# An attention and expert kernel: expert products ahead of the maxima, first-layer tiles in 50 pairs, the second tile table in two parts

## The reference

```python
x = L0_attn_x                                   # (8, 512, 256)
xn = _layernorm(x, axis=-1)
x = x + _L0_attn_ref(xn, ...) + _L0_ffn_ref(xn, ...)
xn = _layernorm(x, axis=-1)
x = x + _L1_attn_ref(xn, ...) + _L1_ffn_ref(xn, ...)
return x
```

## Time and profile before

| what | value |
|---|---|
| median of 3 runs | 3600.68 us (3591.55 to 3601.14) |
| the profiled execution | 3600.47 us, its span 3598.5 us |
| TensorE busy | 2938.4 us, 82% of the span |
| VectorE busy | 2166.3 us, 60% |
| ScalarE, GpSimd busy | 1650.5 us, 1419.2 us |
| 317 to 1560 us | pairs 0 to 51 with the first layer's tiles |
| 1560 to 1708 us | pairs 52 to 63, plain, with the gathers of sequences 0 and 1 |
| 1708 to 2511 us | gqa blocks and the routing of the second layer |
| 2558 to 3419 us | pairs 138 to 177 with the second layer's tiles |

### The profile page before, as it was taken

How to read it: one execution, slowest core, us unless ns; L and a number is a source line. 1 busy time by engine, 2 the same in 40 slices (tenths; PEclk the granted TensorE clock), 3 DMA queues, 4 the chain that set the end, 5 groups by cost and what they waited for, 6 DMA issues and landing times. The chain is left out here.

```text
span 3598.5 us, 61920 instructions
## 1 busy us (share of the span) xinstructions
PE 2938.4 (82%) x21678; PEld 2372.1 (66%) x21678; DVE 2166.3 (60%) x6233; ACT 1650.5 (46%) x3466; POOL 1419.2 (39%) x2037
## 2 busy tenths in 40 slices
PE   4415989898988899878888888987888888888885
PEld 3304778777777787755666666665677777777764
DVE  4534776767766767656777777666444444443465
ACT  1203445444444445445655566555444444444453
POOL 4744424333333424266656565223121212122267
PEclk9998999999999999989999999999999999999999
DMA  8853656555655655522433333211554544444345
GB/s 274 294 190 127 231 187 231 219 223 196 238 212 210 237 207 218 212 71 40 111 83 97 95 96 92 82 67 38 188 187 156 196 166 182 175 173 177 141 95 117
DMA packets 193735, 587.54 MB, mean 163 GB/s; under 512 B 22984, under 2 KB 145808, under 8 KB 158608
## 3 DMA queue, kind: packets, MB, share of 16 engines
q1 hardware_dynamic: 156560, 532.40, 40.1%
q0 software_dynamic: 36864, 51.14, 7.0%
HBM read 456.99 MB, written 126.48 MB: 162 GB/s over the span
## 5 line engine op out<-in xcount | busy, mean ns | idle before, releaser
L1231 POOL TENSOR_TENSOR al<-t,ah 128x512 fp32r<-128x512 f32 x224 | 289.8, 1294 | 1288.8 <-ACT ah L1408 1288.8
L762 PE MATMUL bank<-xh,gu 128*128 128x256 f32 x3584 | 668.8, 292 | 98.6 <-DVE t L1673 93.1
L808 PE MATMUL bank<-masks_bf,ident_bf 128*128 128x128 bf16 (+1 forms) x2304 | 578.6, 251 | 56.9 <-ACT ksT L1490 21.9
L762 PEld LDWEIGHTS bank<-xh,gu 128*128 128x128 f32 x3584 | 531.6, 196 | 118.9 <-DVE t L1673 104.3
L1822 DVE TENSOR_REDUCE st<-bank 128x1 f32<-128x512 f32 (+3 forms) x1024 | 424.4, 481 | 243.1 <-PE bank L815 242.8
L1503 ACT ACTIVATE pt<-bank 128x512 f32<-128x512 f32 (+1 forms) x1152 | 513.2, 540 | 74.3 <-PE bank L818 72.2
L1408 ACT ACTIVATE ah<-t 128x512 fp32r<-128x512 f32 x224 | 141.4, 631 | 714.6 <-DVE t L1666 383.7
L818 PE MATMUL bank<-qaT,ksT 128*128 128x512 f32 (+3 forms) x1536 | 433.3, 390 | 0.0
L1820 DVE MAX8 top<-bank 128x8 f32<-128x512 f32 (+3 forms) x512 | 214.1, 483 | 352.3 <-PE bank L815 352.2
L815 PE MATMUL bank<-ksT,qsT 128*128 128x512 f32 (+3 forms) x1536 | 420.7, 380 | 0.0
L808 PEld LDWEIGHTS bank<-masks_bf,ident_bf 128*128 128x128 bf16 x2304 | 225.4, 98 | 294.1 <-issue 105.7
(11 more groups left out here) (248 smaller groups left out, 5321.4 us busy)
## 6 DMA issues: line engine op xcount, KB each, us to landing
gu<-wu_scratch SPq DMA_DIRECT2D x112, 2056.0 KB, 7.7
dn<-wd_scratch SPq DMA_DIRECT2D x112, 1024.0 KB, 9.5
xs<-xs_scratch SPq DMA_DIRECT2D x112, 264.0 KB, 9.2
ys_scratch<-yb SPq DMA_DIRECT2D x112, 256.0 KB, 9.9
raw<-in_gu SPq DMA_DIRECT2D x16, 1024.0 KB, 10.4
wu_scratch<-hi SPq DMA_DIRECT2D x16, 1024.0 KB, 5.5
wu_scratch<-lo SPq DMA_DIRECT2D x16, 1024.0 KB, 4.0
xs_scratch<-empty SPq DMA_DIRECT2D x32, 264.0 KB, 2.8
```

Source lines behind the costliest of these rows:

```text
L762: mm = pe.matmul(bank[:, TS * h:TS * (h + 1)], gu[:, col:col + P], x[s % 2][:, TS * k:TS * (k + 1)], start=(n == 0), stop=(n == len(terms) ...
L808: pe.matmul(bank[:, diag:diag + P * len(unit)], ident_bf[:, :], masks_bf[:, 0 if which == "q" else 1, 0:len(unit), :].rearrange("p n k -> ...
L1231: pool.tensor_tensor(em["al"][s % 2][:, m, :], em["t"][g % 2][:, :], em["ah"][s % 2][:, m, :].bitcast(F32), ALU.subtract).then_inc(al_read ...
```

## The change

Four things. On VectorE, `finish` no longer stands at the start of a tiled pair but at its end, ahead of `normalize` and `norm_heads`, and once more between slot 2 and `maxima`. The first layer's tiles run in pairs 0 to 49; the gathers of sequence 0 stand in pairs 51 to 54, those of sequence 1 in 55 to 62. The second table's last part (L599 to L608, the slots' compaction) is a function of its own, run in pair 137, and SP waits for the first two of its four steps only. `place` copies its 64 columns of PSUM to SBUF first and works from there, so that the bank is released after the copy.

```diff
-SPANS = ((0, 52), (138, 178))
+SPANS = ((0, 50), (138, 178))
+FIRST_GATHERS = 55
...
     def place(dve, chain, bank, big, k, to, rank_used, slot_ready):
-        before = bank[:, 64:96].rearrange("p (t e) -> p t e", e=E)
-        total = bank[:, 96:128].rearrange("p (t e) -> p t e", e=E)
+        taken = big[:, 1, 128:192]
+        before = taken[:, 0:32].rearrange("p (t e) -> p t e", e=E)
+        total = taken[:, 32:64].rearrange("p (t e) -> p t e", e=E)
+        dve.tensor_copy(taken, bank[:, 64:128]).then_inc(rank_used[0], 1)
         chain(dve.tensor_copy(base[:, 0, :], running[:, :]))
+        dve.wait_ge(*rank_used)
         for t in range(1, NT):
             chain(dve.tensor_tensor(base[:, t, :], base[:, t - 1, :], total[:, t - 1, :], ALU.add))
         chain(dve.tensor_tensor(running[:, :], base[:, NT - 1, :], total[:, NT - 1, :], ALU.add))
-        dve.tensor_tensor(base[:, :, :], before, base[:, :, :], ALU.add).then_inc(rank_used[0], 1)
-        dve.wait_ge(*rank_used)
+        chain(dve.tensor_tensor(base[:, :, :], before, base[:, :, :], ALU.add))
...
         dve.tensor_copy(table[:, 1, :], which[:, 0, :]).then_inc(tabled, 1)
+
+    def compact_slots(dve, chain, layer, scratch, tabled):
...
         chain(dve.tensor_copy(at[:, 0, :], own))
...
-                    sp.wait_ge(tabled, 4)
+                    sp.wait_ge(tabled, 2)
...
-                    if is_at(n + 1, "gqa") and loc(n + 1) == 0:
-                        gather(1, p // 2, p % 2)
-                    if is_at(n + 2, "gqa") and loc(n + 2) == 0 and p >= NP // 2:
+                    if em and ends_at[0] < G <= ends_at[0] + CHOICES[0]:
                         for i in range(2):
-                            gather(0, p - NP // 2, i)
+                            gather(0, G - ends_at[0] - 1, i)
+                    if em and 0 <= G - FIRST_GATHERS < NP:
+                        gather(1, (G - FIRST_GATHERS) // 2, (G - FIRST_GATHERS) % 2)
...
                 def pair_with_experts(G):
                     n, p = divmod(G, NP)
-                    finish()
                     if G:
                         heads_out(G - 1)
...
                     experts(G, 2)
+                    finish()
                     maxima(G + 1, range(NU))
                     shift(G + 1)
                     for q in range(3, 6):
                         experts(G, q)
+                    finish()
                     if is_at(n - 1, "spm") and p == 1:
-                        finish()
                         residual(n - 1)
...
-                    if G + 1 in ends_at:
-                        finish()
...
                         tile_table()
+                    if em and is_at(n - 2, "gqa") and loc(n - 2) == B - 1 and p == 1:
+                        compact_slots(dve, chain, 1, em["scratch"], tabled)
```

More of the change, by code:

```diff
@@ L572, in table_scratch, with tabulate_on @@
         }
-    def tabulate_on(dve, chain, layer, scratch, empty, cleared, tabled):
-        k = CHOICES[layer]
-        own = slots[layer][:, 0:B * NT, :].rearrange("p n k -> p (n k)")
+    def tabulate_on(dve, chain, scratch, empty, cleared, tabled):
         n, over, below, past = (scratch[name] for name in ("n", "over", "below", "past"))
-        which, at, beyond, move = (scratch[name] for name in ("which", "at", "beyond", "move"))
+        which = scratch["which"]
         dve.memset(empty[:, :, :], 0.0).then_inc(cleared, 1)
@@ L598, in tabulate_on @@
         dve.tensor_copy(table[:, 1, :], which[:, 0, :]).then_inc(tabled, 1)
+    def compact_slots(dve, chain, layer, scratch, tabled):
+        k = CHOICES[layer]
+        own = slots[layer][:, 0:B * NT, :].rearrange("p n k -> p (n k)")
+        n, at, beyond, move = (scratch[name] for name in ("n", "at", "beyond", "move"))
         chain(dve.tensor_copy(at[:, 0, :], own))
@@ L620, in _ @@
                 def _(dve):
-                    tabulate_on(dve, Chain(dve, step), layer, scratch, empty, cleared, tabled)
+                    chain = Chain(dve, step)
+                    tabulate_on(dve, chain, scratch, empty, cleared, tabled)
+                    compact_slots(dve, chain, layer, scratch, tabled)
                 @block.sync
@@ L1994, in tile_table @@
                         dve.wait_ge(moved[i], 16 * NP * (B // 2))
-                    tabulate_on(dve, chain, 1, em["scratch"], em["empty"], cleared, tabled)
+                    tabulate_on(dve, chain, em["scratch"], em["empty"], cleared, tabled)
                 def finals(b):
```

## The result

The changed kernel takes 3412.5 us (median of 4 runs, 3407.5 to 3419.2), the kernel before 3600.0 (4 runs, 3591.6 to 3601.1): ratio 0.949, 95% interval 0.946 to 0.951. Forecast were 3431 and a range of 3380 to 3500. The profiled execution has a span of 3409.0 against 3598.5, and a mean granted clock of 0.969 against 0.955.

What follows compares the result with a forecast made beforehand. TensorE's queue was taken as the kernel's clock, with its idle time and lowered clock in the tiled pairs to be won. Terms summed to -169.5 us from 3600.5, giving 3431 us; range 3380 to 3500.

Steps and rivals of the forecast that it cites:

- Product ahead of the maxima, second stretch: Pairs 138 to 177: TensorE's 39 waits of 2.39 us for VectorE's product go, -93 us.
- rival C: Late maxima make shift the wait in the second stretch and 22 first-stretch pairs: +80 us, 3511; chance 0.08.
- Clock there: Second stretch: without the 2.39 us waits the granted clock rises from 0.95 to 0.985, -26 us, bounds 0 and -37.
- Rival A: Idle time goes but the clock stays: 3467 us, or 3490 with half of the first stretch's 47 us; chance 0.20.
- The stretch's last pair: Pair 177: its last product comes ahead of the maxima, so TensorE's wait of 7.06 us goes, -7 us.
- The finish's cost in the second stretch: Finish ahead of normalize delays the next rows' transposes at five block starts, +7 us, bounds 0 and +41.
- First stretch: Product ahead of maxima -31 us, finish ahead of norm_heads -16, clock -10, normalize later at four block starts +8.
- 50 pairs for 52: First-layer tiles in two pairs fewer, gathers a pair earlier: some slow stacks beside gathers, +2 us, bounds -5 and +14.
- Waits that I said would be below 5 us: Sign of being right: TensorE's first-stretch waits on `al` and `yb`, 17.6 and 17.0 us before, fall below 5 us.
- The table in two: Second table's L599 to L608 go behind pair 137's maxima; TensorE's 5.87 us wait ends 3.5 us earlier, -3.5 us.
- place: One more copy frees its bank about 1 us earlier, but the next bank comes 0.2 later: 0, bounds -8 and +2.

Runs made afterwards that it cites:

- finish-only kernel: The kernel before with only the finish moves, ahead of the maxima and at the pair's end; 52 pairs, old gathers, table and place: 3431.0 us, ratio 0.954.

## Why the prediction came out as it did

*Product ahead of the maxima, second stretch (-93): right.* The waits went from 93.1 to 2.4 us. Nothing took their place, since the maxima had their slack and the shift its own. But that slack was read from a pair that doesn't set it: pair 154, at place 2, has a projection ahead of the turn of the shifted queries, which the 0.3 us (0.2 in rival C) leaves out. In the changed kernel there are 2.9 us in such pairs and 0.12 to 0.21 in the 20 pairs without a projection. That the shift was in time there is partly luck. The kernel with the product between maxima and shift and a short `al` shows the other side: rival C was a matter of some 0.6 us, and waits of 0.53 came of it.

*Clock there (-26): right in kind, and 10 us too small.* From shift 138 to 184 the time fell by 134.5 us and TensorE's idle time by 96.2 (foretold: 93); of the other 38.3 about 2.5 are the 15 matmuls that the cut at shift 138 puts on its other side, and the rest, 36, is the clock, near the bound of 37. I had taken it that waits of 1 us would hold it at 0.985. They do not: half clock fell from 88.9 to 10.2 us, and the finish-only kernel has none at all between 139 and 177. Rival A, by which the clock would stay, is refuted: twice over by the line taken out and put in, and by the shorter waits without any fall. With it falls, for this kernel, the rule of the Trainium skill that the prediction weighed (page "TensorE: Matmul & The Clock Gate", section on HAM oscillation), that only gaps longer than these take the clock away. The trace that I set against it, 0.93 in a pair with no longer gap, was the better guide.

*The stretch's last pair (-7): right.* 177 to 184 gave 10.8 us: 7.5 of idle time, the rest clock, of which it had lost 6.8 us at half.

*The finish's cost in the second stretch (+7): too high.* It shows as waits for `xb`, 3.1 us over 5 block starts, where there were none, and 20.3 against 18.5 us for `xl`: 5 at most, inside the 96.2. Against the kernel with the other finish put back the move costs nothing: between 139 and 177 that one has TensorE idle for 26.0 us, the changed kernel for 23.8.

*First stretch (-31, -16, -10, +8) and 50 pairs (+2): the sum right by luck, its parts not.* From 0 to 64 the kernel gained 47.3 us where I had 47. Yet the finish moves alone gave 31.4 there (finish-only kernel, 1359.2 against 1390.6), not 49; the 50 pairs with the gathers alone gave 5.3, not a loss of 2; and both together 10.6 more than the two apart. So the term "50 pairs for 52", +2, was mis-sized: on top of the moved finish it is worth 16. I had counted the two pairs' attention and the gathers but not that the cut of the list decides which pairs end in `up`, and so how many waits there are. The traces show it in the tiled pairs themselves: from shift 0 to the last tiled pair's, 50 pairs take 28.1 us less than 52 with the moved finish (1186.0 against 1214.1), but 14.4 less with the old one (1228.7 against 1243.1), where two pairs' attention is 17.2. The gathers, which I put at 6.3 us of GpSimd less the 6.99 of `row_stats`, are the other part of the 16: 6.8 us by the trace. At 50 pairs I did count the open `up`s, which is why the other terms hold there: the finish ahead of the maxima is worth 28.5 (foretold: 31 and part of the clock), the one ahead of `norm_heads` and `normalize` 19.2 (foretold: 16, less 8 for `normalize`, and the rest of the clock's 10). The two errors, too much for the finish at 52 pairs and too little for the 50 pairs, cancelled. That 48 pairs lose 26.6 us in the same part says the same thing. Which property of the cut is worth how much remains open: I have three cuts and no kernel that changes the order of the items alone.

*Waits that I said would be below 5 us:* `yb` has 5.4 and `al` 9.3, of which 4.2 is the stretch's end. Close, but not met.

*The table in two (-3.5): right in kind, too small.* 136 to 138 went from 36.3 us to 32.9, and 138 to 139 from 30.7 to 25.8. The kernel with the 50 pairs alone has the old table and takes 64.6 us from 136 to 139; the one without the finish ahead of the maxima has the new table and takes 58.7, with the same 13.7 us of half clock. So the term is nearer to -5.9 (these two kernels also differ in the finish at the pair's end and in `place`). The wait for the maxima fell from 5.9 us to 2.0, as foretold; what the sum left out is a wait for GpSimd's stacked keys, 5.4 to 3.3.

*place (0): right within what can be told.* The wait of 11.4 us for L328 became one of 4.7 for the copy, and the next one grew by 5.3, as foretold in kind; from 64 to 136 TensorE's idle time stayed at 99 to 100 us. The 4.2 us of 64 to 136 are inside the 14 us by which that part varies.

The span fell by 20 us more than the sum said (189.5 against 169.5): 10 of it are the clock of the second stretch, 3 its idle time, some 2 to 3 the second table, and 4 the gqa blocks, which vary by more from trace to trace.

## What to carry to other kernels

When one in-order engine serves two chains, look for the instruction whose input has long been there while the engine idles for something else. Moving it into that idle time is free only if what is pushed back has slack, and that slack has to be read from the pair that has the least between the two (0.1 to 0.2 us here in half of the pairs, 2.9 in the others). Price the granted clock with the waits: in the second stretch the waits were worth 96 us of idle time and another 36 through the clock. Before a move, see which engine's later instruction moves with it, since the product put behind the maxima brought GpSimd's subtraction beside one of VectorE's small multiplications and cost 56 us.

## What the runs showed of the hardware that I had not expected

*A small VectorE instruction waits for a GpSimd instruction that began just before it.* A multiplication of 128x64 with both inputs in SBUF takes 0.224 us alone and 1.32 us when it starts 0.04 us behind a GpSimd subtraction of 1.28 us. One of 128x8 takes 0.17 and 1.107. With GpSimd's instruction cut to 0.32 us the first takes 0.36 and the kernel is 56 us faster; of the 57.5 us in the second stretch 35 are idle time and the rest the clock, which came back with the shorter waits. Maxima that read their scores from PSUM were not held: eight take 3.27 us with `al` (2649.93 to 2651.20) under them, and 3.28 without. The Trainium skill, page "SBUF — State Buffer", section "SBUF: two separate sides", says that a VectorE operation with two SBUF inputs and a GpSimd operation that reads SBUF lock a shared pair of ports for a whole instruction, and that the loser waits. The first case and the maxima agree with it. It goes both ways: of the two `norm_heads` multiplications (2.92 us together, 1.83 without `al`) the first took its usual 0.95, `al`, begun 0.22 us behind it, took 1.88 instead of 1.28, and the second, begun inside `al`, took 2.05.

*The clock fell behind one long wait or two shorter ones close together, and not in proportion to the idle time.* In the part from shift 139 to 177, 37 waits of 2.4 us brought 78.5 us of half clock (111.8 us idle in all); 36 waits of about 1.5 us, each by itself, brought none (74.9 idle). It isn't the longest single wait alone: the kernel with the product between maxima and shift had, behind the first pair's 2.4, none above 1.55 us and less idle time (65.5), and yet 54.6 us of half clock. There 19 waits of 1.5 us for the shift were each followed, 0.66 us of work later, by one of 0.66, and 15 of the 16 falls of the clock stand behind such a pair of waits. One of them (timeline of TensorE from 2743 us on, and the busy time and clock of what follows):

```profile
2744.93 0.66 PE L745 MATMUL bank<-ident,qst 128*128 128x128 f32 x4 [1.47 <-DVE qst L1875]
2746.24 1.09 PE L745 MATMUL bank<-ident,oT 128*128 128x128 f32 x4 [0.66 <-ACT qaT L1516]
2746.19:2749.60 3.41, 3.36 (x16) 3.38 (x16) 0.61 (x3) 0.55 (x2) 1.28 (x1) 0.50 0.97 400
```

In the changed kernel two of 19 waits of 1.07 us were followed by a fall, in the finish-only kernel none. With waits of 0.53 and 0.66 us, the same work between them (the short `al`), the clock fell only behind the first pair's 2.4. In between it is open: of the nine waits of 1.94 to 2.12 us for `xl` ahead of the turn of oT in the first stretch of the kernel with the later `norm_heads`, four were followed by 3.4 us of half clock and five were not. No run was made to part the length of a wait from the time between two.
